# A graph network kernel on one core: the attention's probabilities turned by DMA instead of TensorE, s2 as a row from memory, and gather's two halves in two banks

## What is computed

```
s1 = Wh @ a1;  s2 = Wh @ a2
e   = leaky_relu(s1[:, :, None] + s2[:, None, :], 0.2)
att = softmax(where(adj == 0, -inf, e)), then 0 where adj == 0
x   = x1 + att @ Wh
```

## Time and profile before

| | us |
|---|---|
| median of three runs | 1867.82 (1867.44 to 1868.47) |
| the profiled execution, its own time | 1866.37 |
| its span, first to last instruction | 1864.6 |
| granted TensorE clock, mean | 0.993 of full speed |

### The profile page before, as it was taken

One profiled execution on the slowest core, in us unless ns is written; L12 is line 12 of the kernel. 1 busy time (PEld: TensorE's weight loads), 2 busy tenths in 40 slices (PEclk: granted clock), 3 DMA queues, 4 the chain that ended last, 5 costly groups with the idle time before them and its releaser, 6 DMA issues.

```text
span 1864.6 us, 32405 instructions
## 1 busy us (share of the span) xinstructions
PE 1797.0 (96%) x10620; PEld 958.6 (51%) x10620; DVE 1420.2 (76%) x2801; ACT 1028.3 (55%) x1822; POOL 346.5 (19%) x778
## 2 busy tenths in 40 slices
PE   6999999999999999999999999999999999999995
PEld 5444555545555455555545555454554545555453
DVE  6667787777877877877777877777877777877776
ACT  5555555555555546555555556555555555555543
POOL 1022030311303122030310303113031220303101
PEclk9999999999999999999999999999999999999998
DMA  3323232322313223222222313223222322323111
GB/s 103 73 63 69 52 77 48 87 59 56 87 36 90 51 52 88 56 73 51 73 68 51 93 31 101 45 56 90 56 74 45 77 70 51 73 51 84 29 47 51
DMA packets 292000, 120.50 MB, mean 65 GB/s; under 512 B 207489, under 2 KB 291969, under 8 KB 291969
## 3 DMA queue, kind: packets, MB, share of 16 engines
q1 hardware_dynamic: 291968, 120.11, 26.7%
HBM read 52.96 MB, written 16.78 MB: 37 GB/s over the span
## 4 chain that ended last, share of the span: by engine, by line
issue 58%; POOL 13%; DVE 9%; PE 8%; ACT 7%; DMA 3%; POOLq 1%; ACTq 0%; DVEq 0%; SPq 0%
DMA ht_s<-h_s 3%; PE z_bank L318 3%; PE r_bank L318 2%; POOL ln_gnn L310 2%; DVE n_pre L887 2%; POOL ln_att L310 2%; ACT relu_gnn L270 2%; DVE dot_terms L933 1%; PE hn_bank L318 1%; ACT tanh_r L819 1%; PE in_bank L318 1%; ACT relu_att L270 1%; DVE stats_att L248 1%; ACT u_hi L845 1%; POOL ln_att L306 1%
## 5 line engine op out<-in xcount | busy, mean ns | idle before, releaser
L824 ACT ACTIVATE n_out<-n_pre,bih 128x512 f32<-128x512 f32 x192 | 137.9, 718 | 255.0 <-DVE n_pre L887 252.8
L318 PE MATMUL hn_bank<-ht_s,wh_hi 128*128 128x512 f16 x768 | 228.4, 379 | 1.7 <-PEq L426 1.7
L318 PE MATMUL r_bank<-ht_s,wh_hi 128*128 128x512 f16 x768 | 228.4, 379 | 0.0
L318 PE MATMUL z_bank<-ht_s,wh_hi 128*128 128x512 f16 x768 | 228.4, 379 | 0.0
L882 DVE SCALAR_TENSOR_TENSOR n_pre<-tanh_r,hn_b 128x512 f32<-128x512 f32 x192 | 146.2, 761 | 68.1 <-ACT tanh_r L819 65.1
L814 ACT ACTIVATE hn_b<-hn_bank,b_hn,down 128x512 f32<-128x512 f32 x192 | 147.5, 768 | 77.8 <-PE hn_bank L318 77.8
L819 ACT ACTIVATE tanh_r<-r_bank,b_rz,down 128x512 f32<-128x512 f32 x192 | 147.4, 768 | 68.9 <-PE r_bank L318 68.8
L833 ACT ACTIVATE ht_s<-ht 128x512 f16<-128x512 f32 x128 | 80.5, 629 | 186.7 <-DVE ht L903 186.7
L351 DVE TENSOR_TENSOR nb_lo<-nb_bank,nb_hi 128x512 f16<-128x512 f32 x192 | 131.2, 683 | 67.7 <-ACT nb_hi L347 67.6
L295 POOL TENSOR_TENSOR ln_gnn<-stats_gnn 128x4 f32<-128x4 f32 x32 | 12.9, 404 | 901.9 <-DVE stats_gnn L248 901.9
L828 ACT ACTIVATE tanh_z<-z_bank,b_rz,down 128x512 f32<-128x512 f32 x192 | 146.9, 765 | 35.9 <-PE z_bank L318 35.9
(11 more groups left out here) (180 smaller groups left out, 4053.2 us busy)
## 6 DMA issues: line engine op xcount, KB each, us to landing
x_in<-in_x_dram SPq DMA_DIRECT2D x32, 512.0 KB, 4.1
x_res<-in_x_dram SPq DMA_DIRECT2D x32, 512.0 KB, 4.1
out_dram<-x_out SPq DMA_DIRECT2D x32, 512.0 KB, 5.0
adj_in<-in_adj_dram SPq DMA_DIRECT2D x32, 256.0 KB, 4.2
adj_att<-in_adj_dram SPq DMA_DIRECT2D x32, 256.0 KB, 4.3
h_s<-ht_s SPq DMA_TRANSPOSE x128, 3.0
ht_s<-h_s SPq DMA_TRANSPOSE x64, 3.2
raw_ih<-in_L_gnn_w_ih_dram SPq DMA_DIRECT2D x2, 384.0 KB, 3.9
```

The costliest lines, as they stand in the source:

```text
L318: last = nc.tensor.matmul(bank_ap, w, d, start=start and i == 0, stop=stop and i == len(todo) - 1)
L824: nc.scalar.activation(n_out[c][:], n_pre[c][:], ACT.Tanh, bias=bih[:, 4 + c:5 + c]).then_inc(n_ready, 1)
```

## The change

1. **s2 as a row by memory** (all pairs but the last). PE's four transposes of `scores` are gone. SP stores the column s2 of the group (128 x 4 fp32, 2 KB) to a buffer in memory (`store_s2`) and loads it back onto all 128 partitions as s2_row (2 KB each, 256 KB in all, `load_s2`). DVE adds from s2_row, which it reads with a stride of four values, in place of s_bank. The last pair keeps PE's transposes.
2. **Probabilities turned by DMA** (all pairs). ACT and DVE first split prob in SBUF into prob_s (hi and lo, `split_probs`); SP then turns both parts with one DMA transpose into pt_s. PE's `gather` waits for its landing (`pt_landed`).
3. **Gather's second half in its own bank**: t_bank, in place of s_bank. `gather(0, 1)` waits for x1_ready of the last residual, and `residual(0, 0)`, the next user of t_bank, waits for vt_lo_ready of `gather(1, 1)`.
4. **Order.** `gather(1, 0)` moves from (4, 7) and `gather(1, 1)` from (5, 1), both to (5, 0); `residual(0, 0)` from (5, 0) to (5, 1); `scores(1)` from (4, 0) to (4, 1).

```diff
-    (2, 6): [("probs_transpose", 0, -1)],
+    (2, 6): [("split_probs", 0, -1), ("probs_transpose", 0, -1)],
+    (1, 1): [("store_s2", 0, -1)],
+    (1, 3): [("load_s2", 0, -1)],
+    (3, 6): [("store_s2", 1, -1)],
+    (4, 1): [("scores", 1, -1)],
-    (3, 7): [("attend", 0, 1, -1)],
-    (4, 0): [("update", 1, 1, 1, 0), ("split_state", 1, 2, 1, 0), ("transpose", 1, 2, 1, 0), ("scores", 1, -1),
+    (3, 7): [("attend", 0, 1, -1), ("load_s2", 1, -1)],
+    (4, 0): [("update", 1, 1, 1, 0), ("split_state", 1, 2, 1, 0), ("transpose", 1, 2, 1, 0),
-    (4, 5): [("probs_transpose", 1, -1), ("apply_gnn", 0, 1), ("neighbours", 1, 2, 1, 0)],
+    (4, 5): [("split_probs", 1, -1), ("probs_transpose", 1, -1), ("apply_gnn", 0, 1), ("neighbours", 1, 2, 1, 0)],
-    (4, 7): [("gather", 1, 0, -1)],
-    (5, 0): [("residual", 0, 0, 0), ("update", 0, 2, 1, 0)],
-    (5, 1): [("gather", 1, 1, -1)],
+    (5, 0): [("gather", 1, 0, -1), ("gather", 1, 1, -1), ("update", 0, 2, 1, 0)],
+    (5, 1): [("residual", 0, 0, 0)],
...
         def gather_bank(p, half):
-            return r_bank if after_gates(p) and half == 1 else s_bank
+            if half == 0:
+                return s_bank
+            return r_bank if after_gates(p) else t_bank
...
+                def store_s2(p, a):
+                    if not after_gates(p):
+                        sp.wait_ge(dots_ready, per_group(p, a))
+                        sp.dma_start(s2_dram[a], s2[a][:]).then_inc(s2_stored[a], 16)
+
+                def load_s2(p, a):
+                    if not after_gates(p):
+                        sp.wait_ge(s2_stored[a], per_load(p))
+                        wait_reached(sp, sum_ready, per_group(p, a) - 1)
+                        sp.dma_start(s2_row[:].rearrange("q t b -> q (t b)"),
+                                     s2_dram[a].rearrange("t b -> (t b)").unsqueeze(0).broadcast_to(
+                                         [P, T])).then_inc(s2_landed[a], 16)
+
+                def probs_transpose(p, a):
+                    sp.wait_ge(prob_lo_ready, per_group(p, a))
+                    sp.sem_inc(sp_step, 1)
+                    wait_reached(sp, gather_done, per_chunk(p, a, 0) - 1)
+                    sp.sem_inc(sp_step, 1)
+                    sp.dma_start_transpose(pt_s[:].rearrange("p s b t -> p (s b) t"),
+                                           prob_s[:].rearrange("p s b t -> p (s b t)")).then_inc(pt_landed[a], 16)
...
                 def residual(p, a, c):
                     pe.wait_ge(h_ready, per_gate(p, a, LAYERS - 1, c))
                     wait_reached(pe, x1_ready, per_chunk(p, a, c) - 1)
+                    if a == 0 and c == 0:
+                        wait_reached(pe, vt_lo_ready, per_chunk(p - 1, 1, 1))
...
-                def probs_transpose(p, a):
-                    pe.wait_ge(prob_ready, per_group(p, a))
-                    for b in range(GROUP):
-                        last = nc.tensor.transpose(s_bank[:, b * P:(b + 1) * P], prob[:, b, :], ident[:])
-                    last.then_inc(probs_t_done, 1)
...
                 def gather(p, a, half):
                     pe.wait_ge(u_lo_ready, per_group(p, a))
-                    pe.wait_ge(pt_lo_ready, per_group(p, a))
+                    pe.wait_ge(pt_landed[a], per_load(p))
...
+                    elif half == 1 and a == 0:
+                        pe.wait_ge(x1_ready, per_chunk(p, 1, 1))
                     elif half == 1:
-                        pe.wait_ge(vt_lo_ready, n - 1)
+                        pe.wait_ge(vt_lo_ready, n - 2)
...
-                def probs_transpose(p, a):
-                    act.wait_ge(probs_t_done, per_group(p, a))
-                    wait_reached(act, gather_done, per_chunk(p, a, 0) - 1)
-                    nc.scalar.activation(pt_hi[:].rearrange("p b t -> p (b t)"), s_bank[:], ACT.Copy,
-                                         scale=PSCALE).then_inc(pt_hi_ready, 1)
+                def split_probs(p, a):
+                    act.wait_ge(prob_ready, per_group(p, a))
+                    if a == 1:
+                        act.wait_ge(pt_landed[0], per_load(p))
+                    else:
+                        wait_reached(act, pt_landed[1], per_load(p - 1))
+                    nc.scalar.activation(prob_s[:, 0], prob[:], ACT.Copy, scale=PSCALE).then_inc(prob_hi_ready, 1)
...
-                    nc.vector.tensor_tensor(score[:], scores_bank(p, a)[:].rearrange("p (b t) -> p b t", b=GROUP),
-                                            s12[a][:, :, 0:1].broadcast_to([P, GROUP, P]),
+                    nc.vector.tensor_tensor(score[:], row, s1[a][:].unsqueeze(2).broadcast_to([P, GROUP, P]),
                                             ALU.add).then_inc(sum_ready, 1)
...
-                    dve.wait_ge(pt_hi_ready, n)
-                    nc.vector.scalar_tensor_tensor(pt_lo[:].rearrange("p b t -> p (b t)"), s_bank[:], PSCALE,
-                                                   pt_hi[:].rearrange("p b t -> p (b t)"), ALU.mult,
-                                                   ALU.subtract).then_inc(pt_lo_ready, 1)
+                    dve.wait_ge(prob_hi_ready, n)
+                    nc.vector.scalar_tensor_tensor(prob_s[:, 1], prob[:], PSCALE, prob_s[:, 0], ALU.mult,
+                                                   ALU.subtract).then_inc(prob_lo_ready, 1)
```

More of the change, by code:

```diff
@@ L117 @@
 LAST_SLOT_SIDE = {
-    (5, 0): [("residual", 0, 0, 0), ("update", 0, 2, 1, 0)],
-    (5, 1): [("gather", 1, 1, -1), ("attend", 1, 0, -1)],
+    (5, 0): [("gather", 1, 0, -1), ("gather", 1, 1, -1), ("update", 0, 2, 1, 0)],
+    (5, 1): [("residual", 0, 0, 0), ("attend", 1, 0, -1)],
     (5, 2): [("residual", 0, 1, 0), ("stats_att", 0, 0)],
@@ L126 @@
         ("dots", 0, 1), ("scores", 0), ("apply_att", 1), ("split_att", 1), ("softmax", 0), ("dots", 1, 0),
-        ("dots", 1, 1), ("probs_transpose", 0), ("scores", 1), ("gather", 0, 0), ("gather", 0, 1),
-        ("softmax", 1), ("attend", 0, 0), ("probs_transpose", 1), ("attend", 0, 1), ("store", 0), ("gather", 1, 0),
+        ("dots", 1, 1), ("split_probs", 0), ("probs_transpose", 0), ("scores", 1), ("gather", 0, 0), ("gather", 0, 1),
+        ("softmax", 1), ("attend", 0, 0), ("split_probs", 1), ("probs_transpose", 1), ("attend", 0, 1), ("store", 0), ("gather", 1, 0),
         ("gather", 1, 1), ("attend", 1, 0), ("attend", 1, 1), ("store", 1)]
@@ L596, in graph_blocks @@
         u_lo = both("u_lo", [P, GROUP, D], F16)
-        s12 = both("s12", [P, GROUP, 2], F32)
+        s1 = both("s1", [P, GROUP], F32)
+        s2 = both("s2", [P, GROUP], F32)
+        s2_row = sb("s2_row", [P, P, GROUP], F32)
+        s2_dram = [nc.dram_tensor(f"s2_dram{a}", [P, GROUP], F32, kind="Internal").ap() for a in range(2)]
         row_scale = both("row_scale", [P, GROUP], F32)
@@ L610, in graph_blocks @@
         prob = sb("prob", [P, GROUP, P], F32)
-        pt_hi = sb("pt_hi", [P, GROUP, P], F16)
-        pt_lo = sb("pt_lo", [P, GROUP, P], F16)
+        prob_s = sb("prob_s", [P, 2, GROUP, P], F16)
+        pt_s = sb("pt_s", [P, 2, GROUP, P], F16)
         row_max = sb("row_max", [P, GROUP], F32)
@@ L640, in graph_blocks @@
         res_t_done = sem("res_t_done")
-        gather_done, s2_done, probs_t_done, attend_done = (sem("gather_done"), sem("s2_done"), sem("probs_t_done"),
-                                                       sem("attend_done"))
+        gather_done, s2_done, attend_done = sem("gather_done"), sem("s2_done"), sem("attend_done")
+        pt_landed = [sem(f"pt_landed{a}") for a in range(2)]
+        s2_stored = [sem(f"s2_stored{a}") for a in range(2)]
+        s2_landed = [sem(f"s2_landed{a}") for a in range(2)]
         hn_ready, tanh_r_ready, n_ready, tanh_z_ready = (sem("hn_ready"), sem("tanh_r_ready"), sem("n_ready"),
@@ L702, in transpose @@
                                                h_landed[layer - 1][a][c], 16)
+                def store_s2(p, a):
[16 more added lines that the diff above has]
+                                           prob_s[:].rearrange("p s b t -> p (s b t)")).then_inc(pt_landed[a], 16)
                 all_pairs(sp, lambda *step: None, {
                     "load_gnn": lambda p, a: load_gnn(sp, p, a), "store": store, "load_att": load_att,
+                    "probs_transpose": probs_transpose, "store_s2": store_s2, "load_s2": load_s2,
                     "transpose": transpose, "first_transpose": lambda *which: first_transpose_sp(sp, *which)})
@@ L752, in scores @@
                 def scores(p, a):
+                    if not after_gates(p):
+                        return
                     pe.wait_ge(dots_ready, per_group(p, a))
-                    if after_gates(p) and a == 1:
+                    if a == 1:
                         pe.wait_ge(hn_ready, per_gate(p, 1, LAYERS - 1, 1))
@@ L784, in gather @@
                             last = products(target, [(u_hi[a][:, b, cols], u_lo[a][:, b, cols],
```

(19 more changed lines are left out.)

17 lines of the change are left out of this document (10 added, 7 removed).

## The result

The changed kernel takes **1972.73 us** (median of 4 runs, 1970.00 to 1973.13), against 1867.78 us for the kernel before in the same series (1867.44 to 1868.47). The ratio is 1.0558, with an interval of 1.0540 to 1.0577: 105 us slower, where the forecast was 47 us and the range ended at 1942. The profiled execution took 1972.36 us, its span is 1970.6 us, and its mean granted clock is 0.973, before 0.993.

What follows compares the result with a forecast made beforehand. It took new waits of PE, for the probabilities' DMA and for t_bank behind the POOL, ACT and DVE chain, to outweigh PE's savings: 19.0 + 21.6 + 6.5 = +47.1 us on 1866.4, so 1915 us; range 1872 to 1942.

Steps and rivals of the forecast that it cites:

- Part 1: PE's transposes of s2 and probabilities: removing them frees 27.3 us of PE time; with waits, at most 56.7 us to win.
- Part 2: Group 0: PE waits 2.4 us for the probabilities' DMA ahead of gather(0, 0); +1.27 us in 15 pairs, +19.0 us.
- Part 3: Group 1 and t_bank: PE waits 2.6 us ahead of residual(0, 0); in0 +1.54 us later in 14 pairs, +21.6 us.
- Part 4: The tail: no gates hide the DMAs of either group; +6.5 us, bounds +4 and +9.
- The strided row: DVE's scores addition from s2_row at a stride of four: counted at nothing; upper bound 0.69 us in each of 29, +20 us.
- the third rival: TensorE's clock falls in the new waits: 14 to 29 falls of 1.3 us, 1933 to 1953 us; chance 0.10.
- the forecast's two waits: PE's new loop waits: 2.4 us for the DMA ahead of gather(0, 0), 2.6 us for t_bank ahead of residual(0, 0).

Runs made afterwards that it cites:

- e_row: The kernel before with only the s2 row through memory (stores, loads, s2_row); 1879.87 us, ratio 1.0044.
- e_bank: The kernel before with only gather's own bank t_bank and the new order of gather and residual, scores(1) unmoved; 1899.93 us, ratio 1.0149.
- e_stats: The kernel before with one entry moved, stats_gnn of the next pair from (4, 3) to (3, 6); 1841.93 us, ratio 0.9867.
- e_tail: The changed kernel with gather(0, 0), stats_gnn(0), residual(0, 0) moved, PE turning s2 and, in the last pair, the probabilities; 1828.41 us, 0.9788 of the kernel before.
- e_fill: The changed kernel with matmuls whose result is overwritten added ahead of the waits at gather(0, 0) and residual(0, 0); 1931.48 us, 1.0321 of the kernel before.
- e_probs: The kernel before with only its probabilities turned by DMA, gather and residual where they were; 1923.73 us, ratio 1.0287.
- e_g0: The changed kernel with gather(0, 0) moved from (3, 1) to (3, 3); 1920.06 us, 1.0284 of the kernel before.
- e_contig: The changed kernel with s2 stored scattered so that DVE reads the row without a stride; 2077.89 us, 1.1121 of the kernel before.

## Why the prediction was right about the sign and wrong about the size

- **Part 1, PE's savings win nothing: right.** PE waits at `nb_bank` in their place (15.3 us), and e_row shows it alone. Before, this wait was:

```profile
PE nb_bank L332 <- DVE nb_lo L351: 1.4, 2, 1.2
```

- **Part 2: right.** +1.24 us a pair for 1.27, landing 3.0 us.
- **Part 3, mechanism right, size short.** The stretch grew by 2.84 us, not 1.54, and PE waited 3.18 us, not 2.6. Of the excess of 1.30, 0.44 is the clock, 0.38 is the strided addition of group 1, and 0.46 of the remaining 0.48 is, as the timelines read, POOL's longer operation, which the text left out. e_bank and e_stats show the mechanism.
- **Part 4: right**, +6.5 us; e_tail, with PE's transposes back, has 4.2 us of it back in its trace.
- **The strided row, "and nothing is the lower" bound: the value taken was wrong.** It costs 0.38 us in each of 29 rows, 11 us. The bound of 0.69 did hold it. No row of before had such a stride; halfway between the bounds would have been near.
- **The step that failed is the third rival.** "TensorE's clock falls in the new waits" was given 0.10 and kept out of the sum. It is what happened: 24 falls (the text had 14 to 29), at 1.54 to 1.68 us and not 1.3; together 39.8 us, 41 by e_fill. The 1.3 came from 2.6 us of matmuls ahead of the clock's rise in the tail of before, which is read short: PE worked without a pause from 1846.74 to the rise at 1849.7, 3.0 us. The waits of 2.4 and 2.6 us lay between a row that had left the clock alone (1.57 us) and one that had lowered it (3.09 us), nearer to the latter. And it was no other way for the kernel to go: it followed *from* the forecast's two waits, so its price belonged in the sum at even chances, not in a tail of the chances. Even that rival's own top, 1953, fell short of 1972.73, because the stride and POOL stood at nothing beside it. The row of before where PE's work in the tail begins:

```profile
1846.74 1.12 PE L759 MATMUL hn_bank<-ident,s 128*128 128x128 f32 x4 [1.37 <-DVE s L933]
```

By the timeline: 47.1 forecast + 39.8 clock + 11.0 stride + 0.48 x 14 = 6.7 of the residual's stretch is 104.6 us; measured 105. Most terms are one pair's figures times the pairs, so that it closes within 1 us is in part luck.

The Trainium skill ("TensorE: Matmul & The Clock Gate", section "HAM oscillation") warned of this, waits for data in a loop that slow the matmuls behind them, and the prediction cited it. Its example has waits for DMA of 3 to 5 us; here 24 of 29 waits of 2.2 and 3.2 us did the same. That 5 of 15 equal waits left the clock alone is more than its warning tells.

## What to carry to other kernels

A wait that is put into TensorE's path costs its length and the matmuls that run at half clock behind it: here waits of 2.2 us (10 of 15) and 3.2 us brought some 1.6 us each on top, and filler matmuls won that back. Work taken off an engine that is 96% busy is worth nothing where another chain sets the moment at which it may go on; one early start of that chain (e_stats) brought 1.3%, the whole change cost 5.6%. A DMA that others wait for on SP must be short, as all transposes of the loop stand behind that wait.

## What the runs showed of the hardware that was not expected

- Equal waits don't treat the clock equally. The same 2.17-us wait lowered it in 10 pairs and left it alone in every third one of 15; in e_probs it lowered it 14 times of 14. In e_bank waits of 2.85 to 2.90 us left it alone three times, and shorter ones of 2.60 us lowered it. 1.46 us never did, 3.18 us always, in e_g0 too. What tells the spared waits from the others wasn't tried.
- DVE's two-input fp32 addition of 128 x 512 takes 1.07 us with one source at a stride of four values and 0.69 us without. The Trainium skill ("VectorE: DVE Perf Modes", section "Mode 1× (REGULAR) — the baseline") says that the plain mode works with any stride and gives one result per cycle, and names no price for a stride; this case measures one of 0.38 us, and the measurement decides. e_contig shows that it is the stride and not the source in SBUF.
- A store of 2 KB as single 4-byte values held up its reader for 9.57 us; the same 2 KB in order landed in 1.9 us.
- A POOL operation on 128 x 4 values takes 0.20 us, and 0.66 us beside a DVE row of 128 x 512 that reads two tiles in SBUF.
